# A two-layer metaformer on one core: x1 and x2 in a new order, rewritten focal stages, and the attention's normalisation shared between ACT and POOL

## What is computed

```python
# layer 0
x = x + window_attention(_ln_c(x))     # 7x7 windows, shifted by 3; 4 heads of 32; softmax; w_proj
t = tokens(x)
t = t + mixture_of_experts(_ln_t(t))   # 8 experts, best 2 of them
# layer 1
x = from_tokens(t)
x = x + focal(_ln_c(x))
t = t + recurrent(_ln_t(t))            # 3136 steps of y = sigmoid(wx_t + y @ V.T)

def focal(x):
    y = x @ Wf + bf                    # 260 columns: query 128, context 128, 4 gates
    q, ctx, gates = split(y)
    for l, k in enumerate((k0, k1, k2)):           # 3x3, 5x5, 7x7, one filter per channel
        ctx = gelu(dwconv_same(ctx, k)); ctx_all += ctx * gates[..., l:l+1]
    ctx_all += gelu(mean(ctx)) * gates[..., 3:]
    z = q * (ctx_all @ Wh + bh)
    return (layernorm(z, 1e-3) * gamma + beta) @ Wp + bp
```

## Time and profile before

| | us |
|---|---|
| three runs | 10521.58, 10527.13, 10538.14 (median 10527.13) |
| the profiled execution | 10524.25, of it span 10522.5 |
| attention, 0 to 2155 | 2155 |
| experts, 2155 to 4330 | 2175 |
| focal input, 4330 to 5305 | 975 |
| convolution, 5305 to 7150 | 1845 |
| focal output, 7150 to 8650 | 1500 |
| recurrence, 8650 to the end | 1872 |

### The profile page before, as it was taken

One profiled execution on the slowest core, in us unless ns is written; L12 is line 12 of the kernel. 1 busy time (PEld: TensorE's weight loads), 2 busy tenths in 40 slices (PEclk: granted clock), 3 DMA queues, 4 the chain that ended last, 5 costly groups with the idle time before them and its releaser, 6 DMA issues. The chain is left out here.

```text
span 10522.5 us, 333676 instructions
## 1 busy us (share of the span) xinstructions
PE 8609.7 (82%) x109757; PEld 5525.2 (53%) x109757; DVE 6874.4 (65%) x22569; ACT 5282.8 (50%) x14181; POOL 5917.0 (56%) x7369
## 2 busy tenths in 40 slices
PE   7888888878888888677759999995666668888888
PEld 5666666633333333355535555555666655555554
DVE  7888888878888888777725555556778772222222
ACT  4555555545555555566634444444666653333333
POOL 7777777767777777666612222224555554444444
PEclk9999999989999999888879999997888889999999
DMA  1111111111111111498943444437888862222222
GB/s 48 49 49 49 49 49 50 50 48 50 50 48 47 50 50 46 93 178 177 177 135 156 161 158 158 158 129 127 145 142 144 137 110 54 56 56 56 56 56 54
DMA packets 1199080, 961.46 MB, mean 91 GB/s; under 512 B 338169, under 2 KB 1078457, under 8 KB 1190202
## 3 DMA queue, kind: packets, MB, share of 16 engines
q1 hardware_dynamic: 1198522, 956.38, 36.8%
HBM read 576.97 MB, written 455.45 MB: 98 GB/s over the span
## 5 line engine op out<-in xcount | busy, mean ns | idle before, releaser
L943 PE MATMUL moe_pe_out<-moe_we,moe_xnT 128*128 128x512 f32 x3136 | 1531.6, 623 | 373.0 <-DVE moe_odd L836 197.2
L1533 PE MATMUL conv_pc<-conv_c,conv_toep 128*128 128x432 f32 (+1 forms) x3584 | 1370.5, 535 | 0.0
L740 ACT ACTIVATE moe_scaled<-moe_pe_out,moe_gate 128x128 f32<-128x128 f32 x3136 | 891.9, 367 | 867.6 <-PE moe_pe_out L943 865.8
L2092 ACT ACTIVATE rec_yT<-rec_ph 128x32 f32<-128x32 f32 x3136 | 618.5, 197 | 1241.7 <-PE rec_ph L2213 1241.7
L1384 POOL TENSOR_TENSOR conv_g<-conv_c,conv_gate 128x896 f32<-128x896 f32 x128 | 365.1, 2852 | 1462.9 <-DVE conv_out L1496 1362.8
L943 PEld LDWEIGHTS moe_pe_out<-moe_we,moe_xnT 128*128 128x128 f32 x3136 | 557.3, 195 | 1188.3 <-issue 1187.2
L2213 PE MATMUL rec_ph<-rec_yT,rec_vt 128*32 128x32 f32 x25080 | 843.1, 207 | 196.5 <-ACT rec_yT L2092 121.7
L1533 PEld LDWEIGHTS conv_pc<-conv_c,conv_toep 128*128 128x128 f32 x3584 | 672.1, 190 | 599.1 <-issue 599.1
L2139 DVE COPY rec_xT<-rec_pin 128x512 f32<-128x512 f32 x196 | 135.6, 692 | 1240.9 <-PE rec_pin L2185 1240.9
L281 POOL TENSOR_SCALAR att_xn<-att_xin,att_mv,att_rstd 128x128 f32<-128x128 f32 x1024 | 868.2, 857 | 54.1 <-POOL att_rstd L277 54.1
L678 POOL TENSOR_TENSOR moe_paired<-moe_scaled 128x256 f32<-128x256 f32 x784 | 569.3, 726 | 537.2 <-ACT moe_scaled L740 521.5
(11 more groups left out here) (194 smaller groups left out, 21904.3 us busy)
## 6 DMA issues: line engine op xcount, KB each, us to landing
conv_toep<-rows_dram SPq DMA_DIRECT2D x32, 2304.0 KB, 12.6
c<-foc_cs SPq DMA_DIRECT2D x32, 1856.0 KB, 12.0
conv_cin<-c SPq DMA_DIRECT2D x32, 1856.0 KB, 7.5
x<-att_x1s SPq DMA_DIRECT2D x3584, 14.0 KB
ctx_all<-conv_out SPq DMA_DIRECT2D x32, 1792.0 KB, 5.7
att_xin<-x_windows SPq DMA_DIRECT2D x512, 98.0 KB
moe_xin<-x SPq DMA_DIRECT2D x112, 448.0 KB, 3.5
x<-moe_acc SPq DMA_DIRECT2D x112, 448.0 KB, 2.7
```

Source lines behind the costliest of these rows:

```text
L740: ins = act.activation(scaled[:, b, e, :], pe_out[:, b, 1, e * C:(e + 1) * C], ACT.Identity, scale=g)
L943: ins = pe.matmul(pe_out[:, b, half, :], xnT[:, n.slot(2), t, :], we[:, half * 4:half * 4 + 4, :].rearrange("d e c -> d (e c)"), start=Tru ...
L1533: ins = pe.matmul(pc[k][:, half, 0:HALF * wide].rearrange("p (b i) -> p b i", i=wide)[:, :, i0:i1], w, tile[:, n.slot(slots), b, i0 + away ...
L2092: act.activation(yT[:, a, cs], ph[:, a, cs], ACT.Sigmoid).then_inc(moved, 1)
```

## The change

It has four parts.

**x1 and x2 in a new order.** A token's place in DRAM becomes (image, half of the width, band and row of the shifted frame x column within a window, window within the half). Attention then stores a step with 4 DMAs of 49 partitions x 2 runs instead of 14. The focal stages load an image of x2 with 4 DMAs whose runs are 14 KB (`load_quads`): partition = half x row, and tile k holds column k of both halves in the order of the windows.

**Attention.** POOL also makes minus mean times 1/sqrt (two small instructions), normalises two of four tiles and ACT the other two, at the end of ACT's step (norm(n+2)). PE's transposes wait for both. POOL adds the projection's bias one step later, after both.

**Focal input.** 28 tiles of 112 tokens in 7 steps of 4. Two tiles are normalised on POOL and two on ACT; the bias enters as the last row of Wf, with a constant 1 as the last channel. PE transposes, and DVE scatters the transposed tiles from PSUM into one map of the whole image (`spread`, 448 elements a step, rows 256 bytes apart, in one or three instructions). From it PE makes the query with Wf as the weights (one product of 448 columns a step) and context and gates with tiles of two rows as the weights (132 columns). ACT copies both out. q is then stored with channels on partitions, and c0 as [pixel][image][channel], in runs of 12.5 KB and 14.8 KB. Statistics run 11 steps ahead, the scatter 8 ahead; the query of an image needs the scatter of all of it. The load of the image after next is issued behind the stores of the image before.

**Convolution and focal output.** The convolution reads the loaded group directly (no `spread` on ACT); its load has 4096 runs of 464 bytes. The focal output works with channels on partitions: one product with Wh of 448 columns, then three DVE instructions add bh, multiply by q and scatter into yT (`gate`), ACT squares, the layer norm is folded into the projection (a mean column in the weights, a product of the squares with 1/C), DVE applies 1/sqrt in the residual sum (four instructions instead of one), and both 1/sqrt of a step are one POOL instruction of 8 columns (`roots`). x3 is stored in each step with one to three DMAs.

```diff
@@ attention, SP
-                    for r1 in range(WS):
-                        p0 = odd * 64 + r1 * WS
-                        sp.dma_start(dram(x1, n.val(WS * IMG * C, (r1 * IMG + odd * WS) * C),
-                                          [(C, WS), (2 * WS * C, PAIRS), (1, C)]),
-                                     x1s[p0:p0 + WS, n.slot(4), :, :]).then_inc(x1_out[n.slot(4)], 16)
+                    for part in range(2):
+                        at = part * IMG * 28 * C + n.off % 8 * WTOK * 4 * C + odd * C
+                        sp.dma_start(dram(x1, Step(n.loop, 1, n.off // 8).val(PIX * C, at),
+                                          [(4 * C, WTOK), (2 * C, 2), (1, C)]),
+                                     x1s[odd * 64:odd * 64 + WTOK, n.slot(4), 2 * part:2 * part + 2, :])\
...
@@ attention, POOL
-                for t in range(PAIRS):
...
+                for t in range(HERE):
+                    ins = pool.tensor_scalar(xn[:, a, t, :], xin[:, s, t, :], rstd[:, a, t:t + 1],
+                                             nmean[:, a, t:t + 1], ALU.mult, ALU.add)
...
@@ attention, ACT
+                for t in range(HERE, PAIRS):
+                    ins = act.activation(xn[:, a, t, :], xin[:, n.slot(8), t, :], ACT.Identity,
+                                         bias=nmean[:, a, t:t + 1], scale=rstd[:, a, t:t + 1])
+                ins.then_inc(normed_act, 1)
...
                 if last < -1:
                     values(n + 1)
+                if last < -2:
+                    norm(n + 2)
...
@@ attention, PE
                 pe.wait_ge(normed, n.val(1, 1))
+                hold(pe, normed_act, n.val(1, 1), ticks)
...
@@ focal input, POOL, ACT, DVE, PE
+                if last < -10:
+                    scale(n + 10)
+                if last < -9:
+                    norm(n + 9, first + 9)
...
+                query(n, first)
+                if last < -9:
+                    norm(n + 9, first + 9)
+                context(n, first)
...
+                if last < -11:
+                    layer_stats(n + 11, first + 11)
+                if last < -9:
+                    negate(n + 9, first + 9)
+                if last < -8:
+                    spread(n + 8, first + 8)
...
+                query(n, first)
+                context(n, first)
+                if last < -8:
+                    turn(n + 8, first + 8)
...
@@ convolution, ACT and PE
-                act.activation(cch[:, n.slot(4), :, :], cin[:, g.slot(2), :, :, n.off % PER], ACT.Copy).then_inc(spread_out, 1)
...
@@ focal output, POOL, DVE, PE
+                if last < -2:
+                    add_bias(n + 2)
+                roots(n + 1, first + 1)
...
+                if last < -9:
+                    gate(n + 9, first + 9)
+                if first >= 1:
+                    negate(n - 1, first - 1)
+                residual(n)
+                if last < -1:
+                    y_mean(n + 1)
+                x_parts(n)
+                if last < -1:
+                    y_mean_square(n + 1)
+                x_statistics(n)
+                if last < -1:
+                    y_variance(n + 1)
+                x_variance(n)
...
+                if last < -10:
+                    turn_context(n + 10, first + 10)
                 if last < -1:
                     project(n + 1, first + 1)
+                if last < -9:
+                    modulator(n + 9, first + 9)
```

More of the change, by code:

```diff
@@ new lines, in norm, with query @@
+                for t in range(HERE, GRP):
+                    ins = act.activation(xn[:, n.slot(2), t, 0:C - 1], xin[:, m.slot(2), GRP * c + t, 0:C - 1], ACT.Identity,
+                                         bias=nmean[:, a, t:t + 1], scale=rstd[:, a, t:t + 1])
+                ins.then_inc(normed_act, 1)
+            def query(n, first):
+                m, c = image(n)
+                if c == 0 and first >= 2 * NG:
+                    hold(act, q_out[m.slot(2)], m.turn(2, 16), ticks)
+                hold(act, q_made, n.val(1, 1), ticks)
+                at = c * ROWS8 * IMG
+                act.activation(qs[:, m.slot(2), at:at + ROWS8 * IMG], pq[:, n.slot(2), 0:ROWS8 * IMG], ACT.Copy).then_inc(q_read, 1)
@@ new lines, in context @@
+            def context(n, first):
+                m, c = image(n)
+                s = m.slot(2)
+                if c == 0 and first >= 2 * NG:
+                    hold(act, c_out[s], m.turn(2, 16), ticks)
+                    hold(act, g_out[s], m.turn(2, 32), ticks)
+                for i, j, jn in pair_groups(c):
+                    hold(act, c_made, m.val(NG + 1, i + 1), ticks)
+                    act.activation(cs[:, s, :, j:j + jn].rearrange("p c j -> p j c"), py[:, i % 2, 0:jn, 0:C], ACT.Copy)\
+                       .then_inc(c_read, 1)
+                    act.activation(gs[:, s, :, j:j + jn].rearrange("p l j -> p j l"), py[:, i % 2, 0:jn, C:C + 4], ACT.Copy)\
+                       .then_inc(g_read, 1)
@@ L1238, in turn, with query @@
                 ins.then_inc(turned, 1)
+            def query(n, first):
+                m, c = image(n)
+                if c == 0:
+                    hold(pe, xT_out, m.val(NG, NG), ticks)
+                if first >= 2:
+                    hold(pe, q_read, n.val(1, -1), ticks)
+                pe.matmul(pq[:, n.slot(2), 0:ROWS8 * IMG].rearrange("p (r w) -> p r w", w=IMG), wf[:, 0:C],
+                          xnT[:, m.slot(2), 1 + c * ROWS8:1 + (c + 1) * ROWS8, 0:IMG], start=True, stop=True).then_inc(q_made, 1)
@@ new lines, in context @@
+            def context(n, first):
+                m, c = image(n)
+                for i, j0, jn in pair_groups(c):
+                    if first >= 2 or i >= 2:
+                        hold(pe, c_read, m.val(NG + 1, i - 1), ticks)
+                        hold(pe, g_read, m.val(NG + 1, i - 1), ticks)
+                    for j in range(jn):
+                        r = 2 * (j0 + j)
+                        ins = pe.matmul(py[:, i % 2, j, 0:C + 4], xnT[:, m.slot(2), r:r + 2, :].rearrange("p r w -> p (r w)"),
+                                        wf[:, C:OUT], start=True, stop=True)
+                    ins.then_inc(c_made, 1)
@@ L1437, in step @@
                 if first == 0:
-                    for k in range(3):
-                        spread(n + k)
                     gelu(0, n, 0)
@@ L1750, in norm_z @@
+                b, r = n.slot(2), (n + 1).slot(2)
+                for t in range(GRP):
+                    ins = act.activation(z[:, b, t, 0:C], xin[:, m.slot(2), GRP * c + t, :], ACT.Identity,
+                                         bias=nmean[:, b, t:t + 1], scale=rstd[:, r, GRP + t:GRP + t + 1])
                 ins.then_inc(z_normed, 1)
@@ L1912, in project @@
                 ins.then_inc(projected, 1)
             def gram_of(n, first, last):
-                pe.wait_ge(z_normed, n.val(1, 1))
-                for t in range(CH):
+                hold(pe, z_normed, n.val(1, 1), ticks)
+                for t in range(GRP):
                     ins = pe.matmul(pg[:, 0:C + 1], z[:, n.slot(2), t, 0:C], z[:, n.slot(2), t, :],
-                                    start=(first == 0 and t == 0), stop=(last == -1 and t == CH - 1))
+                                    start=(first == 0 and t == 0), stop=(last == -1 and t == GRP - 1))
```

745 lines of the change are left out of this document (350 added, 395 removed).

## The result

| | us |
|---|---|
| before, median | 10530.7 (10521.6 to 10538.1) |
| after, median | 13054.3 (13050.4 to 13063.8) |
| ratio | 1.240, 95% interval 1.238 to 1.242 |
| profiled execution of after | 13050.4, span 13048.7 |

The change makes the kernel 24% slower, 2524 us, where 350 us of gain were forecast. Of the six stages, four have the length that was forecast or nearly so, and the two focal ones have become two to three times as long.

What follows compares the result with a forecast made beforehand. It took SP's issuing to bound the attention, PE the convolution, and chains or waits the focal stages. 10524.25 - 275 - 90 + 5 + 15 = 10179 profiled, so 10180 for the median; range 10040 to 10360.

Steps and rivals of the forecast that it cites:

- The load of an image: Focal input: stores and load of an image, three transfers of 1.6 MB each, take 13.5 us together (12 to 17).
- rival (a): Focal loops gain nothing: transfers take 17 us, an image 29, an output step 6.9; total 10376 or about 10350; chance 0.13.
- The attention: Attention: SP's issuing stops being the limit, DVE is next; a step goes from 8.18 to 7.10 us, saving 275 us.
- SP's price of a store: Attention: each of the 4 stores costs SP 0.45 us, so with the loads SP needs 2.6 us a step.
- The ring of the focal input: Focal input: load waits behind stores, stores behind the last context copy; 13.5 plus 11.5 us, an image 26, saving 90 us.
- The engines' pace: Focal input: without the waits for transfers, POOL's 3.35 us a step would make an image 23.5 us.
- The convolution: Convolution: PE stays the bound at 13.54 us a channel; only the slower first load shows, +5 us.
- The focal output: Focal output: DVE's step goes from 6.42 to 6.45 us, with a longer prologue +15 us; bounds -90 and +130.
- The forecast's wait: Focal output: DVE waits 0.9 us a step for POOL's roots (1.75 us) in front of minus mean.
- Rival (c): Scattered elements cost double in the focal input's scatter and context copy: an image 27.3 us, total about 10220; chance 0.10.
- Rival (e): Focal stages: PE's clock at 1.2 GHz for 0.6 of the time, from denser, shorter bursts; total 10570; chance 0.03.
- Rival (d): Attention is bound by its transfers, not SP's issue, so nothing is gained there; total about 10450; chance 0.03.

Runs made afterwards that it cites:

- e1_48: The kernel after, with each half image of x2 loaded by DMAs of 3, 5 and 48 partitions instead of 3 and 53: 10363.8 us, ratio 0.985 to before.
- e10_pool4: e1_48 plus early image load and the Wh product ahead of the projection on PE, with all four attention tiles normalised on POOL, none on ACT: 10060.0 us.
- e5_early: e1_48, with the focal input's load of the image after next issued ahead of the stores of the image before: 9975.3 us, ratio 0.948 to before.

## Why the prediction was wrong

**The load of an image, the step that failed.** "Three transfers of 1.6 MB each follow: 1.8 MB in large runs landed in 5.7 us ... I take 13.5 us for stores and load together (12 to 17)." The price was taken by bytes and run length, from transfers of other shapes. The load has 53 partitions to a DMA and takes 63.6 us. The same load stands in front of the focal output, where it wasn't costed at all ("-90 ... +130" are bounds of DVE's step). It makes (76.8 - 31.3) x 31.9 = 1451 us in the input, (11.6 - 6.49) x 223 = 1140 in the output; 2591 of the 2690 between after and e1_48, the rest at the stages' starts. No rival held it: (a), with 17 us for the transfers, stayed within the same idea of bytes. The trace of before couldn't show a 53-partition transfer, since its load is cut into 3, 5 and 48, and that odd cut was the sign to ask about. The Trainium skill does state the rule, in "DMA: Bandwidth & Descriptors", section "Why a DMA increments its semaphore by 16 and not by 1": a DMA runs on the largest number of engines up to 16 that divides the slowest dimension of both sides. The runs agree: 48 is fast, 47 and 53 are slow, 51 (three engines) lies between, near its third. The DMA shares agree too, 0.06 with 53 partitions and 0.19 with 51. I weighed the skill's rule on SBUF lines and not this one.

**The attention**: right in kind and nearly in size. 8.18 to 7.15 a step is 264 us, forecast 275. SP's price of a store was mis-sized (0.80 or 0.98 with its gap, not 0.45), and hidden. To ask of ACT's share only that it costs nothing was too little: it saves 0.70 a step (e10_pool4).

**The ring of the focal input**: the right bound, found from the order on SP, and mis-sized at both ends (19.9 instead of 13.5, 13.2 instead of 11.5). With the load mended the stage costs 31.3 us an image, more than the 29.0 of before: a loss of 74 us where a gain of 96 was forecast. That is most of the 184 us between 10180 and e1_48, and it is the half of **rival (a)** that came true; its other half, an output step of 6.9, didn't. The engines' pace was too slow in the sum (23.5, measured 19.4 with the early load). It was POOL's 3.35 a step, in which each of two normalisations stood at 0.82, from the recurrence; here one takes 0.46, and POOL's instructions of a step take 0.23 + 1.04 + 0.90 = 2.2. Why the recurrence's take 0.82 wasn't tested. DVE's minus mean takes 0.16 there, not 1.1: POOL's addition of the query's bias, beside which it ran in the kernel before, is gone.

**The convolution**: +5 forecast; its first to last product takes 1756 us in e1_48 against 1742 in before, 14. PE's reading of the loaded group in place costs 547 ns a product instead of 539.

**The focal output**: 6.49 measured in e1_48 for 6.45 forecast, but by luck. The wait stands ahead of the gate, for PE's product, 1.9 on the mean, instead of ahead of the minus mean, for the roots, 0.9; the sum had no term for PE's order. Against that the minus mean (median 0.62 for 1.15) and the residual (1.11 for 1.36) are shorter. The roots' 1.65 (1.75) and the gate's 1.07 (1.0) are near. The forecast's wait showed, at 0.85 a step, once PE's was gone.

**Rival (c)** was right in the durations: the context copy takes 1.07 us for 512 elements, the scatter 0.93 to 0.95 for 448, where 0.5 to 0.8 and 0.6 stood. They are part of the ring's 13.2 us. **Rival (e)**, the only slower one, named the wrong cause: the granted clock did fall to 0.62 and 0.66, but with PE idle for most of the time. In e1_48 it is 0.79 and 0.77 in the two stages, and in e5_early, with one wait removed and no work taken from PE, 1.00 in the focal input. So the low clock followed the waits. Its price was wrong as well: 0.6 of the time at half speed is a mean clock of 0.7, so that 3.15 becomes at most 4.5, not 5.0, and 4.3 at most 6.1, less than DVE's 6.45; that would have given about 10360. **Rival (d)** is refuted.

## What to carry to other kernels

When a change alters the shape of a transfer, look at its partition count before its bytes: take 48 and 5 rather than 53, and read an odd-looking cut of a load as a price that someone has paid for. A stage in which all engines idle and the DMA share is low, while a single transfer is waited for, is the sign of it. And when a load's buffer is free early, issue the load ahead of the stores: here that was worth 388 us, more than the whole forecast gain.

## What the runs showed of the hardware

- One DMA engine carried 27 GB/s in 14 KB runs while it worked alone (share 0.06), 24 from issue to use (1.52 MB in 63.6 us). How many engines shared a load followed from its partition count: one for 47 and 53, three for 51.
- SP's issue of an attention store had a median of 0.27 to 0.28 us where the two sides divide alike (49 or 28 runs), and of 0.80 to 0.83 where they don't (98 runs, and also the 14 to 42 of the pieces). I hadn't expected that the number of runs matters less than the shape.
- DVE instructions with two inputs in SBUF (minus mean, subtraction of the maximum) were held while POOL's addition over SBUF ran: 0.16 to 0.98 us and 0.98 to 1.89. DVE's statistics, with one input, kept their 0.87 beside the same addition. The Trainium skill says so in "SBUF — State Buffer", section "Who interferes with whom": a DVE instruction with two SBUF inputs contends with a GpSimd one that reads SBUF. The rows agree in all three cases for POOL's addition over 512 columns. Beside POOL's power over 4 columns, which reads SBUF too, no hold is seen: a DVE multiplication with two inputs in SBUF keeps its 0.98 us (e10_pool4, 1004.18, the power runs from 1003.52 to 1004.56).
- A power on POOL takes 0.58 us for one column, 1.04 for 4 (both in the kernel before) and 1.65 for 8: 0.43 fixed and 0.15 a column. The first two, in the trace of before, give 1.65 for the roots; the prediction took 1.75.
